# Local attention on one core: masks of the second scoring moved from matrix products into spare rows and GpSimd selects

## The chip, the core and the metric

One Trainium2 chip; the kernel uses 1 of its cores. The metric is the device time of one execution in microseconds. The engines are TensorE (PE, with its weight loads as PEld), VectorE (DVE), ScalarE (ACT), GpSimd (POOL), and SyncE (SP), which issues the DMAs here. The engines run on their own and meet at semaphores.

## The reference

A sequence of 4096 tokens of width 256 goes through a global causal attention on one side and two layers of "local attention, then gated MLP" on the other; the two results are multiplied. Only the local attention changes. Cut to what matters (4096 tokens, 8 heads of 64, a window of 128):

```python
def local_attention(q, k, v):                  # once in each of 2 layers
    w = n // WINDOW
    bq = q.reshape(b, h, w, WINDOW, d) * QK_SCALE
    ...
    bk, bv = (look_around(bk), look_around(bv))        # previous and own window
    sim = jnp.einsum('bhwid,bhwjd->bhwij', bq, bk)
    mask = (i < j) | (i > j + WINDOW) | (j == -1)
    sim = jnp.where(mask, -jnp.finfo(sim.dtype).max, sim)
    attn = jax.nn.softmax(sim, axis=-1)
    out = jnp.einsum('bhwij,bhwjd->bhwid', attn, bv)
```

A query sees its own window up to itself, and of the window before it the part from the same offset on. So each window of keys is seen by two windows of queries, each through a triangle.

## The kernel before

`local_attention_layer` holds everything that changes. It works on 16 pairs of windows (32 windows of 128 tokens, `NT`), in a hand-written software pipeline: every engine runs `for k in range(NI + 4)`, and in iteration k it works on several stages of different pairs. The order in which the calls stand in each engine's loop is the order in which that engine runs them; only semaphores tie the engines together.

Scores are made twice. `score_max(w)` makes them with queries on partitions: a mask by four products of an identity with a stored mask (`mask_unit`, L1094: 128x512 bf16, one for each of four PSUM banks of `SU`), then the query-key products (L1109). DVE's `row_max` takes the maxima (L1315) and writes their negative in two parts, high and low, to `msp` (L1323, L1325); PE transposes `msp` (L1147), ACT copies the result to `negm` (L1020). `score_turned(kb)` makes the scores again with keys on partitions, for the two query windows that see key window kb: again `mask_unit`, then products of `row1` with `negm` (L1126), which add the negative maxima, and then the query-key products (L1133). ACT takes the exponential to `PT` (`weights`, L1012), two instructions for each window, for four heads each. PE's `weigh` multiplies `PT` with `V` and with ones (L1211).

The products of `score_max` and `score_turned` use 32 of PE's 128 rows each, four of them side by side. In `msp` each group of 32 rows after the transpose holds the two parts of the maxima and 30 rows of zeros; `row1` has ones in the first two rows of each group and zeros in the rest. The windows are stored in a ring of six (`RW = 6`), so the two query windows of kb are next to each other except when kb modulo 6 is 5; then `spans` splits the products into two runs.

One iteration has two halves. In the **odd half** PE runs score_max(2k-3), the transposes of the input (L1226), weigh(k-4, 1), score_turned(2k-5), a broadcast (L1242), the transpose of the maxima (L1147), values(2k) (L75 to L77 into B6) and then the output projection (L75 to L77 with `woh`). That last one waits for ACT's copy of the values out of B6 (L1027) and for POOL's `oTl` (L974). In the **even half** it runs the query and key projections, score_max(2k-2), more projections, values(2k+1), score_turned(2k-4), the sums of squares (L1277), the transpose of the maxima, the transposes of the sums (L1285, which wait for ACT's copy `sse`, L1081), and weigh(k-3, 0).

DVE runs in the odd half: the maxima (L1315), L1323, L1325, a copy of one column (L1365) and a subtraction (L1368), then the reciprocal (L1348) and the product `on` (L1352) for the pair k-4, and the scaling of queries and keys (L1379). ACT follows: the high part of `on` (L1040), the two exponentials of window 2k-5, `negm`, and the copy of the values. POOL has `low_part` (L974, a subtraction), the four rotary additions (L987) and the power (L993); in time, the power of iteration k is followed by low_part(k-3, 0), and in iteration k+1 by low_part(k-3, 1).

Of the kernel before, what the change touches and what calls it, by code (L numbers as in the profile page):

```python
# [6 lines left out]
F32 = mybir.dt.float32  # L7
# [6 lines left out]
P = 128  # L14
# [853 lines left out]

def local_attention_layer(nc, layer, X, w_qkv, w_o, rope, scale_cols, ident, identb, window_mask):

    with ExitStack() as ctx:
# [22 lines left out]
        ones = sb("ones", [P, HQ])  # L895
        row1 = sb("row1", [P, P], F32R)
        tab = sb("tab", [P, 4, N2])
# [15 lines left out]
        on = sb("on", [P, OC, N2])  # L913
        oT_hi, oT_lo = (sb(f"oT{i}", [P, OC, N2], F32R) for i in "hl")
        stage = PT[:, 0:2, :, :].rearrange("p a b c -> p (a b c)")

# [3 lines left out]
        B7 = psum("B7", [P, 512])  # L920

        const_in, wq_in, wo_in = sem("const_in"), sem("wq_in"), sem("wo_in")
        wh_done, wl_done, set_done, nsc_done = sem("wh_done"), sem("wl_done"), sem("set_done"), sem("nsc_done")
# [8 lines left out]
        def live(k):  # L932
            return 0 <= k < NI
# [15 lines left out]
        @block.sync  # L949
        def _(sp):  # L950
            sp.dma_start(stage[:, 0:EC * 3 * INNER], w_qkv).then_inc(wq_in, 16)
            for dst, src in ((id_sb[:, :], ident), (idb_sb[:, :], identb), (mask[:, :], window_mask), (sc_sb[:, :], scale_cols)):
                sp.dma_start(dst, src).then_inc(const_in, 16)
            sp.wait_ge(wh_done, 1)
            sp.wait_ge(wl_done, 1)
            sp.dma_start(stage[:, 0:OC * E], w_o).then_inc(wo_in, 16)
            for k in range(NI):
                if k >= 1:
                    sp.wait_ge(rope_done, 16 * k)
                sp.dma_start(tab[:, :, :], rope[:, k, :, :]).then_inc(tab_in, 16)  # L960

        @block.gpsimd
        def _(pool):
            pool.memset(half[:, :], -0.5).then_inc(half_set, 1)
            pool.memset(msp[:, :, :, :, :].rearrange("p a b c d -> p (a b c d)").bitcast(F32), 0.0).then_inc(set_done, 1)
            pool.memset(ones[:, :], 1.0).then_inc(set_done, 1)
            pool.wait_ge(half_set, 1)

            def low_part(p, q):
                if live(p):  # L970
                    pool.wait_ge(ohi_done, 2 * p + q + 1)
                    if p >= 1:
# [4 lines left out]
                                       ).then_inc(olo_done, 1)  # L977

            for k in range(NI + 4):
                low_part(k - 4, 1)  # L980
                if live(k):
                    for g in range(4):
                        n = 4 * k + g
                        pool.wait_ge(rope_done, 4 * (n + 1))
                        if k >= 1:
                            pool.wait_ge(nrm_done, 2 * (k - 1) + g // 2 + 1)
                        pool.tensor_tensor(rot[:, g, :, :].rearrange("p a b -> p (a b)"),  # L987
                                           t[:, n % 2, 0, :, :].rearrange("p a b -> p (a b)"),
                                           t[:, n % 2, 1, :, :].rearrange("p a b -> p (a b)"), ALU.add).then_inc(rot_done, 1)
                    pool.wait_ge(ssc_done, k + 1)  # L990
                    if k >= 1:
                        pool.wait_ge(rnx_done, k)
                    pool.tensor_tensor(rn[:, :, :, :].rearrange("p a b c -> p (a b c)"),  # L993
                                       ssc[:, :, :, :].rearrange("p a b c -> p (a b c)"), half[:, :], ALU.pow).then_inc(rn_done, 1)
                low_part(k - 3, 0)

        @block.scalar
        def _(act):
# [4 lines left out]
            act.wait_ge(wl_done, 2)  # L1003
            act.wait_ge(set_done, 10)

# [80 lines left out]
        def _(pe):  # L1086
            pe.wait_ge(const_in, 64)
            pe.wait_ge(wh_done, 2)
            pe.wait_ge(wl_done, 2)
            pe.wait_ge(set_done, 10)  # L1090

# [22 lines left out]
            def score_turned(kb):  # L1114
# [72 lines left out]
            def weigh(p, q):  # L1187
# [103 lines left out]
        def _(dve):  # L1291
            dve.memset(blocks[:, :], 0.0).then_inc(clear_done, 1)
            dve.memset(row1[:, :].bitcast(F32), 0.0).then_inc(clear_done, 1)
            dve.wait_ge(clear_done, 2)
            for i in range(4):
                dve.memset(blocks[32 * i:32 * i + 32, i:i + 1], 1.0).then_inc(set_done, 1)
                dve.memset(row1[32 * i:32 * i + 2, :].bitcast(F32), 1.0).then_inc(set_done, 1)
# [3 lines left out]
            dve.wait_ge(const_in, 64)  # L1301
            dve.tensor_scalar(nsc[:, :], sc_sb[:, :], -1.0, None, ALU.mult).then_inc(nsc_done, 1)
            dve.wait_ge(wh_done, 2)
# [3 lines left out]
            dve.wait_ge(set_done, 10)  # L1307

# [384 lines left out]
def build(nc, t, out, stop=99):  # L1693
# [17 lines left out]
    for layer in range(DEPTH):  # L1711
        n = str(layer)
        local_attention_layer(nc, layer, X, t["w_lqkv" + n], t["w_lo" + n], t["rope"], t["rope_scale" + n], t["ident"],
                              t["identb"].bitcast(BF16), t["window_mask"].bitcast(BF16))
        mlp_layer(nc, layer, X, t["w_1" + n], t["w_2" + n], t["b_1" + n], t["ln" + n], t["b_2" + n], t["ident"],
                  t["shift"], t["carry"])
# [3 lines left out]
def lay_out(inp):  # L1720
# [58 lines left out]
    both = np.concatenate([np.where(c < r, MASKED, 0.0), np.where(c > r, MASKED, 0.0)], 1)  # L1779
    arr["window_mask"] = bf16_bits(np.tile(both, (1, 2)))  # L1780
    arr["shift"] = (c == r + 1).astype(np.float32)
    arr["carry"] = ((r == P - 1) & (c == 0)).astype(np.float32)
# [14 lines left out]
```

## Time and profile before

| | |
|---|---|
| time, median of 3 runs | 3600.45 us (3595.33 to 3605.28) |
| the profiled execution | 3591.3 us, of which its span is 3589.6 us |
| PE busy | 88% |
| DVE busy | 66% |
| ACT busy | 48% |
| POOL busy | 22% |
| first local attention, from the load of its weights to the load of the MLP's | 1783.8 to 2391.6 us |
| its steady loop | about 34.5 us for one of the iterations 4 to 15 |

The page gives each engine's busy share. In its 40 slices the local attention stands in slices 20 to 26 and 30 to 36. A timeline lists the instructions of an engine in order of time: start, length, engine, line, operation, tiles, shapes, how many were merged into the row, and in brackets how long the engine was idle before it and who ended that. Records of matmuls can be missing: of 512 mask products 386 are in the trace.

### The profile page before, as it was taken

Reading aid. Unit: us, or ns where it says so; the run is one execution under the profiler, and the core shown is the slowest. Engines: PE = TensorE matmul, PEld = TensorE weight load, DVE = VectorE, ACT = ScalarE, POOL = GpSimd, SP = SyncE. Lnnn points to the kernel's source line nnn. Section 1 sums busy time; section 2 is a strip of 40 time slices with the busy share of each in tenths; the row PEclk is TensorE's granted clock in tenths of the full one; section 3 lists DMA queues with packets and bytes.
Section 4 is the critical chain, followed back from the end, with each engine's and each line's share of the span. In section 5 each row is a group of like instructions: output and inputs, shape, how many; then the busy total and the mean of one; then the engine's idle time right before and its main releaser. Section 6 shows DMA issues by size and latency. Waiting matters only on the chain. (4 is left out here: it accounts for less than half of the span.)

```text
span 3589.6 us, 75899 instructions
## 1 busy us (share of the span) xinstructions
PE 3172.1 (88%) x31726; PEld 1932.4 (54%) x31852; DVE 2376.7 (66%) x3284; ACT 1724.8 (48%) x3173; POOL 783.9 (22%) x757
## 2 busy tenths in 40 slices
PE   7799999999999999999679999959978999985995
PEld 6333333334433333333457777747766777764884
DVE  7698978987889977765246655635545556654554
ACT  4266777887678778777123333212213333321222
POOL 8410000000100000001034343302224333331221
PEclk9699999999999999989789999979989999997998
DMA  7420001000200000000310000000000000000003
GB/s 246 128 53 16 9 9 44 9 16 17 66 24 9 16 9 4 5 7 8 128 30 19 13 20 19 8 31 0 0 32 19 19 20 13 19 8 31 0 0 141
DMA packets 62014, 113.62 MB, mean 32 GB/s; under 512 B 9608, under 2 KB 25480, under 8 KB 61192
## 3 DMA queue, kind: packets, MB, share of 16 engines
q1 hardware_dynamic: 57608, 102.84, 9.3%
q10 hardware_dynamic: 4096, 6.30, 0.7%
q8 instruction: 237, 3.88, 0.5%
q14 instruction: 73, 0.60, 0.1%
HBM read 74.77 MB, written 33.55 MB: 30 GB/s over the span
## 5 line engine op out<-in xcount | busy, mean ns | idle before, releaser
L647 DVE TENSOR_REDUCE mp<-ps_m 128x2 f32<-128x1024 f32 (+3 forms) x1152 | 1281.1, 1134 | 245.4 <-PE ps_m L698 182.8
L623 ACT ACTIVATE probs<-ps_s 128x512 f32<-128x512 f32 (+3 forms) x2304 | 1161.5, 560 | 395.9 <-PE ps_s L722 366.3
L738 PE MATMUL ps_o<-probs,vall 128*32 128x256 f32 (+3 forms) x9216 | 715.6, 383 | 13.4 <-POOL probs L602 12.6
L722 PE MATMUL ps_s<-qst,kst 64*128 64x512 f32 (+3 forms) x2304 | 611.0, 491 | 39.0 <-ACT probs L623 23.7
L722 PEld LDWEIGHTS ps_s<-qst,kst 64*128 64x128 f32 x2304 | 243.3, 188 | 507.9 <-ACT probs L623 444.5
L698 PE MATMUL ps_m<-kst,qst 64*128 64x512 f32 (+3 forms) x2304 | 485.7, 400 | 31.7 <-DVE mp L647 14.1
L738 PEld LDWEIGHTS ps_o<-probs,vall 128*32 128x32 f32 x9216 | 186.6, 109 | 343.1 <-issue 207.8
L698 PEld LDWEIGHTS ps_m<-kst,qst 64*128 64x128 f32 x2304 | 236.7, 193 | 72.5 <-DVE mp L647 53.6
L987 POOL TENSOR_TENSOR a_rot<-a_t 128x512 f32<-128x512 f32 x128 | 163.0, 1274 | 448.0 <-DVE a_t L1342 448.0
L591 POOL TENSOR_TENSOR msplit<-negm,mzero 128x16 fp32r<-128x16 f32 x32 | 7.2, 224 | 1136.3 <-DVE negm L653 1136.3
L1512 ACT ACTIVATE m_gl<-m_bank_u,m_b 128x512 f32<-128x512 f32 x96 | 66.1, 688 | 345.0 <-PE m_bank_u L77 345.0
L1033 ACT ACTIVATE a_sq<-a_BP 128x512 f32<-128x512 f32 x128 | 76.6, 598 | 292.1 <-PE a_BP L77 292.1
L1342 DVE SCALAR_TENSOR_TENSOR a_t<-a_BP,a_sc,a_tab 128x256 f32<-128x256 f32 x384 | 166.8, 476 | 62.6 <-ACT a_sq L1033 62.4
L993 POOL TENSOR_TENSOR a_rn<-a_ssc,a_half 128x32 f32<-128x32 f32 x32 | 174.0, 5438 | 94.2 <-DVE a_ssc L1399 94.2
L1040 ACT ACTIVATE a_oTh<-a_on 128x512 fp32r<-128x512 f32 x64 | 40.4, 631 | 300.1 <-DVE a_on L1352 300.1
L75 PE MATMUL m_bank_u<-m_hh,m_w1h 128*128 128x512 f32 x384 | 156.0, 406 | 28.3 <-DVE m_uf L1619 28.3
L1348 DVE RECIPROCAL a_rec<-a_B 128x256 f32<-128x256 f32 x64 | 112.2, 1754 | 100.3 <-PE a_B L1211 99.8
L1315 DVE TENSOR_REDUCE a_mx<-a_SU 128x4 f32<-128x1024 f32 (+1 forms) x128 | 148.6, 1202 | 39.2 <-PE a_SU L1109 39.2
L602 POOL TENSOR_SCALAR_AFFINE_SELECT probs<-probs 128x256 f32<-128x256 f32 x256 | 101.9, 406 | 331.2 <-ACT probs L623 331.1
L1012 ACT ACTIVATE a_PT<-a_SU 128x1024 f32<-128x1024 f32 (+1 forms) x128 | 122.4, 1008 | 106.1 <-PE a_SU L1133 106.1
L1491 POOL TENSOR_TENSOR m_ul<-m_uf,m_uh 128x512 fp32r<-128x512 f32 x96 | 126.2, 1315 | 195.0 <-DVE m_uh L1625 195.0
L76 PE MATMUL m_bank_u<-m_hl,m_w1h 128*128 128x512 f32 x384 | 153.0, 398 | 0.0
(182 smaller groups left out, 5241.2 us busy)
## 6 DMA issues: line engine op xcount, KB each, us to landing
a_tab<-in_rope SPq DMA_DIRECT2D x32, 512.0 KB
q_parts<-pparts SPq DMA_DIRECT2D x32, 256.0 KB, 3.9
k_parts<-pparts SPq DMA_DIRECT2D x32, 256.0 KB, 3.8
qst<-q_parts SPq DMA_DIRECT2D x64, 128.0 KB, 2.7
o_raw<-o_sb SPq DMA_DIRECT2D x32, 256.0 KB, 2.0
X<-in_x SPq DMA_DIRECT2D x8, 512.0 KB, 7.3
kst<-k_parts SPq DMA_DIRECT2D x32, 128.0 KB, 3.7
qst<-q_parts SPq DMA_DIRECT2D x64, 64.0 KB, 2.6
```

What stands on the lines that cost most here:

```text
L75: pe.matmul(out, a_hi, b_hi, start=start, stop=False)
L76: pe.matmul(out, a_hi, b_lo, start=False, stop=False)
L623: act.activation(probs[:, s % PR, h, off:C], sslots[n % SR][:, off:C], ACT.Exp, scale=float(D) ** -0.5).then_inc(exp_done, 1)
L647: dve.tensor_reduce(mp[b % 2][:, h:h + 2, cc:cc + 1], slot[:, :, 0:width], AX.X, ALU.max).then_inc(max_read, 1)
L698: last = pe.matmul(slot[:, x, 0:width], qst[q_slot(b)][rows, hp, a * P:(a + 1) * P], kst[g % 2][rows, hp, cc * C:cc * C + width], start=Tr ...
L722: pe.matmul(sslots[n % SR][:, off:C], kst[g % 2][rows, hp, i * P:(i + 1) * P], qst[q_slot(b)][rows, hp, off:C], start=True, stop=True).the ...
L738: last = pe.matmul(ps_o[32 * h:32 * h + VW, lo:hi], vall[:, i, (g * GH + h) * DV:(g * GH + h) * DV + VW], probs[:, s % PR, h, lo:hi], star ...
L987: pool.tensor_tensor(rot[:, g, :, :].rearrange("p a b -> p (a b)"), t[:, n % 2, 0, :, :].rearrange("p a b -> p (a b)"), t[:, n % 2, 1, :, ...
L993: pool.tensor_tensor(rn[:, :, :, :].rearrange("p a b c -> p (a b c)"), ssc[:, :, :, :].rearrange("p a b c -> p (a b c)"), half[:, :], ALU. ...
L1315: dve.tensor_reduce(mx[:, w % 2, 2 * b:2 * b + 2, :], SU[:, 2 * b:2 * b + 2, :].rearrange("p i (q c) -> p i q c", q=2)[:, :, :, lo:N2], AX ...
L1342: dve.scalar_tensor_tensor(out=dst, in0=src, scalar=s, in1=table, op0=ALU.mult, op1=ALU.mult).then_inc(rope_done, 1)
L1491: pool.tensor_tensor(u_lo[:, m, :], uf[:, m % 2, :], u_hi[:, m, :].bitcast(F32), ALU.subtract).then_inc(ul_done, 1)
```

## The change

`score_turned` no longer calls `mask_unit`. Three things take its place.

- A staircase mask in the rows that were zero. A new table comes in by one more DMA. `msp` is no longer set to zero but to a table whose columns 2 to 17 hold -1e30 where the query's block of eight tokens matches the column; after the transpose these are 16 more rows beside the maxima in `negm`. `row1` becomes two stationary operands: `rows_own` for the key's own window and `rows_next` for the next one, with ones in rows 2 to 17 where a key's block of eight lies wholly on the masked side. Since the two differ, the product is made per query window: 16 products of 128 columns where there were 8 of 256 (where the ring split them there were 16 of 128 already). The first of them in each bank starts the accumulation.
- What the staircase leaves, triangles of eight by eight, is set to zero after the exponential by GpSimd: `trim(kb, b)` is two affine_selects on 128x512 elements each, in place in `PT` (one in the last window).
- `weigh` waits for `trim_done`, which counts these selects.

`score_max` keeps its mask. The setup loses a memset on POOL and five on DVE and gains three copies on DVE.

```diff
@@ the loads
             for dst, src in ((id_sb[:, :], ident), (idb_sb[:, :], identb), (mask[:, :], window_mask), (sc_sb[:, :], scale_cols),
+                             (table, window_rows)):
@@ gpsimd
+            def trim(kb, b):
+                if win(kb):
+                    pool.wait_ge(exp_done, 2 * kb + b + 1)
+                    part = PT[:, kb % PR, 2 * b:2 * b + 2, :].rearrange("p i (q c) -> p (i q) c", q=2)
+                    own = pool.affine_select(part[:, :, 0:P], part[:, :, 0:P], pattern=[[0, 4], [1, P]], compare_op=ALU.is_ge,
+                                             fill=0.0, base=0, channel_multiplier=-1)
+                    own.then_inc(trim_done, 1)
+                    if kb + 1 < NT:
+                        pool.affine_select(part[:, :, P:N2], part[:, :, P:N2], pattern=[[0, 4], [-1, P]], compare_op=ALU.is_ge,
+                                           fill=0.0, base=0, channel_multiplier=1).then_inc(trim_done, 1)
             for k in range(NI + 4):
                 low_part(k - 4, 1)
+                trim(2 * k - 6, 1)
+                trim(2 * k - 5, 0)
                 if live(k):
                     for g in range(4):
+                        if g == 2:
+                            trim(2 * k - 5, 1)
...
+                else:
+                    trim(2 * k - 5, 1)
+                trim(2 * k - 4, 0)
                 low_part(k - 3, 0)
@@ tensor
             def score_turned(kb):
...
-                mask_unit()
-                for q in range(2):
-                    for at, off, n in runs:
+                for part, rows_by in enumerate((rows_own, rows_next)[0:2 if kb + 1 < NT else 1]):
+                    at = ((kb + part) % RW) * P
+                    for q in range(2):
                         for i in range(4):
                             rows = slice(32 * i, 32 * i + 32)
-                            pe.matmul(SU[:, i, q * N2 + off:q * N2 + off + n], row1[rows, :], negm[rows, q, at:at + n],
-                                      start=False, stop=False, tile_position=(32 * i, 0), skip_group_check=True)
+                            pe.matmul(SU[:, i, q * N2 + part * P:q * N2 + part * P + P], rows_by[rows, :], negm[rows, q, at:at + P],
+                                      start=(part == 0 and q == 0), stop=False, tile_position=(32 * i, 0), skip_group_check=True)
@@ weigh
                     pe.wait_ge(exp_done, 2 * (2 * p + 2))
+                    pe.wait_ge(trim_done, min(4 * (2 * p + 2), 4 * NT - 2))
@@ vector, setup
+            dve.tensor_copy(rows_own[:, :], table[:, 0:P]).then_inc(set_done, 1)
+            dve.tensor_copy(rows_next[:, :], table[:, P:2 * P]).then_inc(set_done, 1)
+            dve.tensor_copy(msp[:, :, :, :, :].rearrange("p a b c d -> p (a b c) d"), ...
```

On PE, at the score_turned of an even half, between the last products of the values and the first of weigh, there stands before:

```order
L77 MATMUL a_B<-a_wqh,a_hTl 128x512
L1094 MATMUL a_SU<-a_mask,a_idb 128x512 x4
L1126 MATMUL a_SU<-a_negm,a_row 128x256 x8
L1133 MATMUL a_SU<-a_QK 128x256 x16
L1277 MATMUL a_B<-a_sq,a_blocks 32x256 x8
L1147 MATMUL a_B<-a_id,a_msp 128x128 x2
L1285 MATMUL a_B<-a_id,a_sse 128x128 x2
```

and now, with rowso for `rows_own` and rowsn for `rows_next`:

```order
L77 MATMUL a_B<-a_wqh,a_hTl 128x512
L1146 MATMUL a_SU<-a_negm,a_rowso 128x128 x8
L1146 MATMUL a_SU<-a_negm,a_rowsn 128x128 x8
L1153 MATMUL a_SU<-a_QK 128x256 x16
L1298 MATMUL a_B<-a_sq,a_blocks 32x256 x8
L1167 MATMUL a_B<-a_id,a_msp 128x128 x2
L1306 MATMUL a_B<-a_id,a_sse 128x128 x2
```

The four mask products are gone and the row products are twice as many at half the width; nothing else on PE moved.

On POOL, from the low parts of one iteration of the steady loop to the rotary additions of the one after the next, it read before:

```order
L974 TENSOR_TENSOR a_oTl<-a_on,a_oTh 128x512 x2
L987 TENSOR_TENSOR a_rot<-a_t 128x512 x4
L993 TENSOR_TENSOR a_rn<-a_ssc,a_half 128x32
L974 TENSOR_TENSOR a_oTl<-a_on,a_oTh 128x512 x2
L987 TENSOR_TENSOR a_rot<-a_t 128x512 x4
```

and one iteration reads now:

```order
L1004 TENSOR_TENSOR a_rot<-a_t 128x512 x2
L1010 TENSOR_TENSOR a_rn<-a_ssc,a_half 128x32
L985 AFFINE_SELECT a_PT<-a_PT 128x4x128
L989 AFFINE_SELECT a_PT<-a_PT 128x4x128
L976 TENSOR_TENSOR a_oTl<-a_on,a_oTh 128x512 x2
L985 AFFINE_SELECT a_PT<-a_PT 128x4x128
L989 AFFINE_SELECT a_PT<-a_PT 128x4x128
L985 AFFINE_SELECT a_PT<-a_PT 128x4x128
L989 AFFINE_SELECT a_PT<-a_PT 128x4x128
L1004 TENSOR_TENSOR a_rot<-a_t 128x512 x2
L985 AFFINE_SELECT a_PT<-a_PT 128x4x128
L989 AFFINE_SELECT a_PT<-a_PT 128x4x128
```

Two selects came between the power and the low parts, four between the low parts and the rotary additions, and two between the second and the third of these.

## Rows read from the trace of the kernel before

**Rows 1.** Busy time by stage: PE, PEld, DVE, ACT, POOL, then granted clock, DMA, GB/s

```profile
1835.00:2283.00 448.00, 414.84 (x5486) 320.04 (x5536) 264.61 (x452) 143.46 (x234) 175.27 (x92) 1.00 0.06 18
...
2723.00:3170.00 447.00, 413.84 (x5465) 319.03 (x5511) 263.72 (x450) 144.83 (x235) 174.61 (x92) 1.00 0.06 18
```

**Rows 2.** One line by itself, the mask products: ns of one, min/median/max

```profile
L1094 PE MATMUL a_SU<-a_mask,a_idb x386: 379/379/389, 1834.3 to 3252.8; 128*128 128x512 bf16 x193
```

**Rows 3.** Timeline, even half, PE then ACT: start, us long, engine, line [idle before]

```profile
2029.05 0.81 PE L1094 MATMUL a_SU<-a_mask,a_idb 128*128 128x512 bf16 x3
2029.79 0.51 PE L1126 MATMUL a_SU<-a_negm,a_row 32*128 32x256 f32 x8
2030.13 1.89 PE L1133 MATMUL a_SU<-a_QK 32*128 32x256 f32 x32
2034.37 0.44 PE L1285 MATMUL a_B<-a_id,a_sse 128*128 128x128 f32 x2 [0.98 <-ACT a_sse L1081]
...
2032.10 1.94 ACT L1012 ACTIVATE a_PT<-a_SU 128x1024 f32<-128x1024 f32 x2 [2.49 <-PE a_SU L1133]
2033.93 0.39 ACT L1081 ACTIVATE a_sse<-a_B 128x256 f32<-128x256 f32 x1
```

**Rows 4.** Timeline, odd half, PE

```profile
2044.69 0.67 PE L1126 MATMUL a_SU<-a_negm,a_row 32*128 32x128 f32 x16
...
2045.19 2.00 PE L1133 MATMUL a_SU<-a_QK 32*128 32x128 f32 x64
...
2050.60 0.36 PE L75 MATMUL a_B<-a_woh,a_oTh 128*128 128x256 f32 x1 [0.78 <-ACT a_V L1027]
```

**Rows 5.** Timeline, odd half: DVE, ACT and POOL, in order of time

```profile
2035.12 5.44 POOL L993 TENSOR_TENSOR a_rn<-a_ssc,a_half 128x32 f32<-128x32 f32 x1 [3.21 <-DVE a_ssc L1399]
...
2040.53 2.36 DVE L1315 TENSOR_REDUCE a_mx<-a_SU 128x4 f32<-128x1024 f32 x2 [0.43 <-PE a_SU L1109]
...
2040.85 1.27 POOL L974 TENSOR_TENSOR a_oTl<-a_on,a_oTh 128x512 fp32r<-128x512 f32 x1 [0.29 <-ACT a_oTh L1040]
...
2042.92 0.18 DVE L1323 TENSOR_SCALAR a_msp<-a_mx 128x8 fp32r<-128x8 f32 x1
...
2043.13 0.17 DVE L1325 SCALAR_TENSOR_TENSOR a_msp<-a_mx,a_msp 128x8 fp32r<-128x8 f32 x1
...
2043.91 1.75 DVE L1348 RECIPROCAL a_rec<-a_B 128x256 f32<-128x256 f32 x1
...
2049.10 0.39 ACT L1020 ACTIVATE a_negm<-a_B 128x256 fp32r<-128x256 f32 x1
...
2049.86 0.60 ACT L1027 ACTIVATE a_V<-a_B 128x512 f32<-128x512 f32 x1 [0.37 <-PE a_B L77]
```

**Rows 6.** One line by itself, POOL: the selects of the global attention, ns min/median/max

```profile
L602 POOL TENSOR_SCALAR_AFFINE_SELECT probs<-probs x256: 403/406/416, 159.2 to 1716.7; 128x256 f32<-128x256 f32 x128
```

**Rows 7.** Groups by line, POOL: the rotary additions (count, busy, mean ns, idle before)

```profile
L987 POOL TENSOR_TENSOR a_rot<-a_t 128x512 f32<-128x512 f32 x128 | 163.0, 1274 | 448.0 <-DVE a_t L1342 448.0
```

**Rows 8.** Timeline, inner loop of the MLP: DVE copies beside a GpSimd subtraction

```profile
2445.53 0.43 DVE L1625 CAST m_uh<-m_uf 128x512 fp32r<-128x512 f32 x1
...
2445.93 1.85 DVE L1632 CAST m_hh<-m_hf 128x512 fp32r<-128x512 f32 x2
...
2446.03 1.46 POOL L1491 TENSOR_TENSOR m_ul<-m_uf,m_uh 128x512 fp32r<-128x512 f32 x1 [1.50 <-DVE m_uh L1625]
```

**Rows 9.** Timeline, third iteration: the same DVE steps beside the power

```profile
1843.67 5.44 POOL L993 TENSOR_TENSOR a_rn<-a_ssc,a_half 128x32 f32<-128x32 f32 x1 [0.65 <-DVE a_ssc L1399]
...
1848.63 0.18 DVE L1323 TENSOR_SCALAR a_msp<-a_mx 128x8 fp32r<-128x8 f32 x1
```

**Rows 10.** Timeline, drain, PE

```profile
2353.83 0.38 PE L75 MATMUL a_B<-a_woh,a_oTh 128*128 128x256 f32 x1 [0.84 <-POOL a_oTl L974]
```

**Rows 11.** Timeline, start of the first layer: the weights from issue to use

```profile
1783.75 0.33 SPq L951 DMA_DIRECT2D a_PT<-in_w_lqkv  x1
...
1790.43 2.76 ACT L1000 ACTIVATE a_wqh<-a_PT 128x3072 fp32r<-128x3072 f32 x1 [64.99 <-DMA a_PT<-in_w_lqkv]
```

More of the change, by code:

```diff
@@ L866, in _, with local_attention_layer @@
                                       bo_sb[:, :].rearrange("p (o e) -> p o e", o=1).broadcast_to([P, 2, E]), ALU.add).then_inc(y_out, 1)
-def local_attention_layer(nc, layer, X, w_qkv, w_o, rope, scale_cols, ident, identb, window_mask):
+def local_attention_layer(nc, layer, X, w_qkv, w_o, rope, scale_cols, ident, identb, window_mask, window_rows):
     with ExitStack() as ctx:
@@ L895, in local_attention_layer @@
         ones = sb("ones", [P, HQ])
-        row1 = sb("row1", [P, P], F32R)
+        rows_own, rows_next = (sb(f"rows{i}", [P, P], F32R) for i in "on")
         tab = sb("tab", [P, 4, N2])
@@ L914, in local_attention_layer @@
         oT_hi, oT_lo = (sb(f"oT{i}", [P, OC, N2], F32R) for i in "hl")
+        table = sq[:, 0, :, :].rearrange("p a b -> p (a b)")[:, 0:2 * P + HQ]
         stage = PT[:, 0:2, :, :].rearrange("p a b c -> p (a b c)")
@@ L920, in local_attention_layer @@
         B7 = psum("B7", [P, 512])
+        trim_done = sem("trim")
         const_in, wq_in, wo_in = sem("const_in"), sem("wq_in"), sem("wo_in")
@@ L951, in _ @@
             sp.dma_start(stage[:, 0:EC * 3 * INNER], w_qkv).then_inc(wq_in, 16)
-            for dst, src in ((id_sb[:, :], ident), (idb_sb[:, :], identb), (mask[:, :], window_mask), (sc_sb[:, :], scale_cols)):
+            for dst, src in ((id_sb[:, :], ident), (idb_sb[:, :], identb), (mask[:, :], window_mask), (sc_sb[:, :], scale_cols),
+                             (table, window_rows)):
                 sp.dma_start(dst, src).then_inc(const_in, 16)
@@ L1003, in _ @@
             act.wait_ge(wl_done, 2)
-            act.wait_ge(set_done, 10)
+            act.wait_ge(set_done, 8)
             def weights(kb):
@@ L1086, in _ @@
         def _(pe):
-            pe.wait_ge(const_in, 64)
+            pe.wait_ge(const_in, 80)
             pe.wait_ge(wh_done, 2)
             pe.wait_ge(wl_done, 2)
-            pe.wait_ge(set_done, 10)
+            pe.wait_ge(set_done, 8)
             def mask_unit():
@@ L1292, in _ @@
             dve.memset(blocks[:, :], 0.0).then_inc(clear_done, 1)
[L1293 to L1294 removed]
+            dve.wait_ge(clear_done, 1)
             for i in range(4):
                 dve.memset(blocks[32 * i:32 * i + 32, i:i + 1], 1.0).then_inc(set_done, 1)
[L1297 removed]
             dve.wait_ge(wh_done, 1)
@@ L1300, in _ @@
                               wq_hi[:, :, :].rearrange("p a b -> p (a b)").bitcast(F32), ALU.subtract).then_inc(wl_done, 1)
-            dve.wait_ge(const_in, 64)
+            dve.wait_ge(const_in, 80)
             dve.tensor_scalar(nsc[:, :], sc_sb[:, :], -1.0, None, ALU.mult).then_inc(nsc_done, 1)
+            dve.tensor_copy(rows_own[:, :], table[:, 0:P]).then_inc(set_done, 1)
+            dve.tensor_copy(rows_next[:, :], table[:, P:2 * P]).then_inc(set_done, 1)
+            dve.tensor_copy(msp[:, :, :, :, :].rearrange("p a b c d -> p (a b c) d"),
+                            table[:, 2 * P:2 * P + HQ].rearrange("p (o d) -> p o d", o=1).broadcast_to([P, 16, HQ])
+                            ).then_inc(set_done, 1)
             dve.wait_ge(wh_done, 2)
@@ L1306, in _ @@
             dve.wait_ge(nsc_done, 1)
-            dve.wait_ge(set_done, 10)
+            dve.wait_ge(set_done, 8)
             def row_max(w):
@@ L1780, in lay_out @@
     arr["window_mask"] = bf16_bits(np.tile(both, (1, 2)))
+    block = np.arange(P) // 8
+    rows_own, rows_next = np.zeros((32, P), np.float32), np.zeros((32, P), np.float32)
+    rows_own[0:2], rows_next[0:2] = 1.0, 1.0
+    rows_own[2:18] = block[None, :] > np.arange(16)[:, None]
+    rows_next[2:18] = block[None, :] < np.arange(16)[:, None]
+    hot = np.zeros((P, 32), np.float32)
+    hot[:, 2:18] = np.where(block[:, None] == np.arange(16)[None, :], MASKED, 0.0)
+    arr["window_rows"] = np.ascontiguousarray(np.concatenate([np.tile(rows_own, (4, 1)), np.tile(rows_next, (4, 1)), hot], axis=1))
     arr["shift"] = (c == r + 1).astype(np.float32)
```

3 lines of the change are left out of this document (1 added, 2 removed).

## Prediction

> **What bounds the kernel now.** The page's first section first, whose shares stand in the table of the time before: PE 88%, no other engine over 66%. The busy table by stage says it more sharply for the two loops that the change touches: PE is busy 415 of 448 us in one and 414 of 447 us in the other, at a granted clock of 1.00 all through, with DVE at 264 and POOL at 175 us [rows 1]. So these loops are PE's, and what leaves PE's queue counts, but only where nothing else is waited for right behind it. That the busy table can't say; the timeline of one iteration can. In the even half PE runs without a gap into score_turned and then stops for 0.98 us for ACT's copy `sse`; ACT itself stood idle for 2.49 us until score_turned ended, then ran two exponentials and that copy [rows 3]. That pause therefore hangs on the end of score_turned and moves with it. In the odd half PE stops for 0.78 us ahead of the output projection, for ACT's copy of the values [rows 4]. Here ACT comes from elsewhere: DVE's maxima start at 2040.53, the reciprocal at 2043.91, `negm` on ACT ends at 2049.49, and the copy of the values starts at 2049.86, having waited 0.37 us for PE [rows 5]. Between, ACT takes the high part of DVE's product ahead of the exponentials, so its queue is fed by DVE and not by score_turned. This chain starts with score_max, ahead of the edit.
>
> **What leaves PE.** Three recorded mask products take 0.81 us, and one takes 0.379 [rows 2, 3], so they follow each other every (0.81 - 0.379) / 2 = 0.2155 us, and four are 0.86 us. The fourth isn't in the record; the row products start 0.74 us after the first recorded one [rows 3], which is three steps and 0.09 us of change-over, and the change-over stays. The row products grow from 8 of 256 columns, 0.34 us from 2029.79 to 2030.13 [rows 3], to 16 of 128; the trace has that shape too, where the ring splits them: 0.50 us from 2044.69 to 2045.19 [rows 4]. That is 0.16 us more (none for the five odd windows that are split already). Net: 0.70 us less PE for each score_turned.
>
> **The even half** gets all of it. Exponentials, `sse` and its transposes come 0.70 us earlier, since ACT was idle. There are 16 such windows in a layer (0, 2, ... 30): 16 x 0.70 = 11.2 us.
>
> **The odd half** gets little. PE comes 0.70 us earlier to its wait, but the copy of the values can start at best when ACT is free, 0.37 us earlier [rows 5]. The rest becomes pause: 0.78 + 0.33 = 1.11 us. This holds for the 12 windows 3 to 25. Window 1 has no such wait and gets 0.70. Windows 27, 29 and 31 get nothing: in the drain PE waits there for POOL's `oTl`, 0.84 us in the one shown [rows 10], at the end of the same DVE chain.
>
> **What POOL gets.** A select of 128x256 takes 406 ns [rows 6]. The new ones have twice the elements, so 0.81 us if it scales from zero and some 0.71 if 0.1 us of it is fixed (an estimate); I take 0.76. The far bound is the subtraction of the same 512 elements with two inputs, 1.27 us [rows 5]. Eight of them are 6.1 us in an iteration of 34.5 in which POOL has 175/448 = 39% of busy time [rows 1]: there is room, so the question is only the place of each. The pair between the rotary additions and the four behind the low parts stand ahead of additions that wait for DVE anyway, 448 us for 128 of them or 3.5 us each [rows 7]; the even half's `weigh` asks for selects that stand two additions ahead of the power, so long done. They cost nothing as long as four of them, 3 us, fit between the low parts and the first addition, and if they didn't, each us too many would delay DVE's use of its two `t` buffers. The first pair is different. It goes between the power, which ends at 2035.12 + 5.44 = 2040.56, and low_part(k-3, 0), which ran from 2040.85 to 2042.12 [rows 5]. With the pair ahead of it low_part ends at 2040.56 + 2 x 0.76 + 1.27 = 2043.35, with the gaps between some 2043.4. Nobody waits for this low part so early. But DVE's small steps L1323 and L1325 start at 2042.92 and 2043.13 [rows 5], until now just behind it, and now beside it.
>
> Do DVE's SBUF steps stand still beside a GpSimd operation? In the MLP, yes: a copy of 128x512 takes 0.43 us, and two of them beside a GpSimd subtraction of 1.46 us took 1.85 instead of 0.86; the last one began where that subtraction ended, at about 2047.4 [rows 8]. Beside the power, no: L1323 took its 0.18 us there [rows 9]. The low part is a subtraction like the one in the MLP, so I take the held case: L1323 begins at 2043.4 and not at 2042.92, and DVE's chain, the one that bounds the odd half, is 0.45 us late (0.38 to 0.58 with selects of 0.71 to 0.81; 0 if not held). The Trainium skill states this as a rule that speaks against the change (SBUF — State Buffer, section "SBUF: two separate sides"): the port pair that VectorE and GpSimd share is an exclusive lock held for a whole instruction, and it is taken by a DVE instruction in a two-port mode or, against a GpSimd instruction that reads SBUF, by one with two SBUF inputs. 
>
> So the odd half comes to 0.37 - 0.45 = -0.08 us: 12 x -0.08 = -1.0, window 1 gives +0.7, and window 27, where the power is still there in the drain, loses about 0.3. Sum of the odd half: -0.6 us a layer.
>
> **Setup.** The three DVE copies (128x512 at most, so each under the 0.43 us of rows 8 and its like) stand where DVE waits for the load of `w_o`, and so cost nothing; without that cover it would be 1 us a layer. The added DMA is 0.15 MB behind the 1.57 MB of `w_lqkv`, which took 6.7 us from issue to use [rows 11]: 0 if they go one after the other, 9% of 6.7 = 0.6 us if they share. I take 0.25 us a layer.
>
> **The sum.** A layer: 11.2 - 0.6 - 0.25 = 10.3 us; two layers: 20.7 us. Against the profiled execution: 3591.3 - 20.7 = 3570.6. That execution was 9 us under the median of the runs, so against the median: 3600.45 - 20.7 = 3580, which is 0.6% faster. What measurement can tell from no change here is about 0.3%, 11 us.
>
> **Rival 1: DVE is not held.** Tiny steps slip through as beside the power. Then the odd half keeps its 0.37: 13 x 0.45 = 5.9 us more a layer, 3568. For it: rows 9. Against it: rows 8.
>
> **Rival 2, the other side: the first pair of selects is long.** Four separate rows of 128 with a stride may run like a two-input operation. Place: between the power and low_part(k-3, 0); price: each select counts twice, 26 times in two layers, through DVE's held chain, so 0.1 us more of length costs 5.2 us. At 1.27 us low_part ends at 2044.4, DVE is 1.47 us late, and the sum is -20.7 + 26 x 1.02 = +6: 3606. It decides from 0.76 + 20.7/52 = 1.16 us on. Against it: rows 7, an operation of the same kind on two such rows. Half way to it, selects of 0.95 to 1.08 us give 3580 + 52 x (0.19 to 0.32) = 3590 to 3597.
>
> **Rival 3: the clock.** The pause ahead of the output projection grows from 0.78 to 1.1, with the hold 1.6 us. The granted clock was 1.00 through both loops with pauses of 0.8 and 1.0 us in each iteration [rows 1, 3, 4]. If it fell to 1.2 GHz now, 20.7 / 24 = 0.86 us of PE work at that level in each steady iteration would eat the gain; a few times that much gives 3620. The Trainium skill (TensorE: Matmul & The Clock Gate, "A second HAM failure mode: psum-queue depth-cycling") tells of short idle spells between groups of matmuls that make the clock swing between its two levels. By that rule the time would be this rival's; the rows at 1.00 so far speak against it.
>
> **That the even half's gain is hidden** is the last one: some later DVE or POOL step bounds it after all. I find none, since ACT's 2.49 us of idleness is ended by PE, but it would leave only the odd half and the setup: 3600 + 2 x 0.85 = 3602.
>
> **Chances.** Forecast (3574 to 3587) 0.50; rival 1 0.22; rival 2 0.06 in full and 0.09 half way; rival 3 0.04; even gain hidden or lost elsewhere 0.09. The range is 3560 to 3597: it takes in the forecast, rival 1 with some noise below it, and rival 2 half way. Faster by over 0.3% (under 3590): 0.76. Within: 0.15. Slower: 0.09.
>
> **What would show it.** In the new profile: 256 mask products left instead of 512 (fewer are recorded); score_turned 0.70 us shorter; the pause ahead of the output projection 1.1 us or more, that ahead of `sse` unchanged at 0.98; selects of 0.71 to 0.81 us; L1323 in the odd half beginning where low_part(k-3, 0) ends; the clock at 1.00. The iteration would be 0.6 us shorter (held) or 1.07 (not held). I am wrong if PE waits for `trim_done` anywhere, if selects pass 1.1 us, or if DVE's reciprocal begins as early after the maxima as before (3.38 us from 2040.53 to 2043.91).

## The result and the profile after

The changed kernel takes 3562.43 us (median of 6 runs, 3556.87 to 3576.12) where the one before took 3601.64 (6 runs, 3595.33 to 3605.28). The ratio is 0.9899, with a 95% interval of 0.9880 to 0.9919: faster by 1.0%, or 29 to 43 us. The prediction was 3580 us in a range of 3560 to 3597. The direction holds, and the time lies in the range by 2 us; the gain is almost twice the 20.7 us forecast, and the time lies nearer to rival 1 (3568). The profiled execution took 3556.87 us, 34.4 less than the one of before.

The page's head and the busy table of the same stretches as [rows 1] come first (columns as there):

```profile
span 3555.1 us, 76617 instructions
...
PE 3139.6 (88%) x32012; PEld 1927.2 (54%) x32012; DVE 2378.4 (67%) x3280; ACT 1720.0 (48%) x3173; POOL 931.3 (26%) x1007
```

```profile
1835.00:2283.00 448.00, 416.54 (x5786) 328.86 (x5788) 275.08 (x466) 148.03 (x244) 238.15 (x196) 1.00 0.06 18
2723.00:3170.00 447.00, 418.93 (x5887) 330.40 (x5889) 272.85 (x460) 148.58 (x243) 238.66 (x198) 1.00 0.06 17
```

PE's share is what it was, the granted clock is 1.00 in both loops, so rival 3 is out, and of the columns only POOL's has moved much, from 175 to 238 us (DVE's by some 10). Since the share doesn't tell where the time went, the timelines have to. First the even half on PE, to be laid beside [rows 3]:

```profile
2021.68 0.45 PE L1146 MATMUL a_SU<-a_negm,a_rowso 32*128 32x128 f32 x8
2021.95 0.39 PE L1146 MATMUL a_SU<-a_negm,a_rowsn 32*128 32x128 f32 x8
2022.18 1.95 PE L1153 MATMUL a_SU<-a_QK 32*128 32x256 f32 x32
...
2026.47 0.33 PE L1306 MATMUL a_B<-a_id,a_sse 128*128 128x128 f32 x1 [0.98 <-ACT a_sse L1101]
```

No mask products, row products of 0.50 us, and the same pause of 0.98 us behind. Then the odd half, for [rows 4] and [rows 5]: PE, DVE, POOL and ACT, each in order of time.

```profile
2035.82 0.45 PE L1146 MATMUL a_SU<-a_negm,a_rowso 32*128 32x128 f32 x8
...
2041.87 0.36 PE L75 MATMUL a_B<-a_woh,a_oTh 128*128 128x256 f32 x1 [0.92 <-ACT a_V L1047]
...
2032.63 2.36 DVE L1339 TENSOR_REDUCE a_mx<-a_SU 128x4 f32<-128x1024 f32 x2 [0.42 <-PE a_SU L1129]
2035.02 0.17 DVE L1347 TENSOR_SCALAR a_msp<-a_mx 128x8 fp32r<-128x8 f32 x1
2035.23 0.17 DVE L1349 SCALAR_TENSOR_TENSOR a_msp<-a_mx,a_msp 128x8 fp32r<-128x8 f32 x1
...
2036.00 1.75 DVE L1372 RECIPROCAL a_rec<-a_B 128x256 f32<-128x256 f32 x1
...
2032.62 0.63 POOL L985 TENSOR_SCALAR_AFFINE_SELECT a_PT<-a_PT 128x512 f32<-128x512 f32 x1
2033.21 0.63 POOL L989 TENSOR_SCALAR_AFFINE_SELECT a_PT<-a_PT 128x512 f32<-128x512 f32 x1
2033.81 1.28 POOL L976 TENSOR_TENSOR a_oTl<-a_on,a_oTh 128x512 fp32r<-128x512 f32 x1
...
2039.05 1.92 ACT L1032 ACTIVATE a_PT<-a_SU 128x1024 f32<-128x1024 f32 x2
2040.86 0.38 ACT L1040 ACTIVATE a_negm<-a_B 128x256 fp32r<-128x256 f32 x1
2041.12 0.61 ACT L1047 ACTIVATE a_V<-a_B 128x512 f32<-128x512 f32 x1
```

Three things are to be seen. A select takes 0.63 us and the next one starts after 0.59, so the record of the low part ends at 2033.81 + 1.28 = 2035.09. DVE's L1347 starts at 2035.02, 0.07 us before that end, and takes its usual 0.17 us: of the 0.45 us that the forecast priced nothing is left (in iterations 5 to 14 the two lie 0.04 to 0.10 us over each other). The reciprocal comes 3.37 us after the maxima, as before (3.38), which the prediction had named as a sign that it is wrong. And the copy of the values now starts 0.26 us after `negm` does, without waiting for PE; PE idles 0.92 us for it, against 0.78.

Measured by the starts of the power, one of which stands in each iteration, the steady iteration fell from 34.63 to 33.28 us (22 intervals in the two layers, of the iterations 4 to 15), by 1.35 us. PE's rows split this: from the output projection to the sums of squares (even) 16.15 to 15.47 us, so -0.68; from the first query-key product of score_max to the output projection (odd) 11.99 to 11.32, so -0.67; the stretch between them stays at 6.5. The forecast had -0.70 and +0.08.

### The profile page after: what moved, and what is told of

Read it like the earlier page. It is cut to its first block and busy times, and to the rows that moved or that the text cites. A ratio compares the mean times of both kernels' runs of the same rounds, so it can differ in the third digit from the quotient of the medians.

```text
span 3555.1 us, 76617 instructions
## 1 busy us (share of the span) xinstructions
PE 3139.6 (88%) x32012; PEld 1927.2 (54%) x32012; DVE 2378.4 (67%) x3280; ACT 1720.0 (48%) x3173; POOL 931.3 (26%) x1007
## 5 line engine op out<-in xcount | busy, mean ns | idle before, releaser
L1339 DVE TENSOR_REDUCE a_mx<-a_SU 128x4 f32<-128x1024 f32 (+1 forms) x128 | 148.7, 1203 | 39.2 <-PE a_SU L1129 39.2
```

Of the source, the lines that this page charges most:

```text
L1339: dve.tensor_reduce(mx[:, w % 2, 2 * b:2 * b + 2, :], SU[:, 2 * b:2 * b + 2, :].rearrange("p i (q c) -> p i q c", q=2)[:, :, :, lo:N2], AX ...
```

## Experiments

The table has the level of each: the steady iteration, the sum over both layers of the time from the first power to the sixteenth, and the ratio to the kernel before in runs on the same chip. Columns two and three come from the one profiled execution, and leave out the global attention ahead, which no kernel here touches and which is the larger part of the scatter: the load of the first layer's weights, behind it, is issued anywhere from 1777.4 (e10_pair_late) to 1809.2 us (e8_stair_pair_late).

| kernel | iteration, us | both layers, us | ratio to before (95%) |
|---|---|---|---|
| before | 34.63 | 983.0 | |
| changed | 33.28 | 952.7 | 0.9899 (0.9880 to 0.9919) |
| after_again | 33.28 | 948.8 | 0.9917 (0.9887 to 0.9946) |
| e1_mask_even | 34.16 | 976.0 | 0.9995 (0.9978 to 1.0011) |
| e2_mask_odd | 34.10 | 970.6 | 0.9977 (0.9963 to 0.9992) |
| e3_selects_only | 34.62 | 983.6 | 1.0028 (1.0011 to 1.0046) |
| e4_pair_twice | 34.39 | 979.6 | 1.0002 (0.9982 to 1.0021) |
| e5_v_first | 33.12 | 946.6 | 0.9916 (0.9884 to 0.9949) |
| e6_stair_max | 32.62 | 932.7 | 0.9868 (0.9838 to 0.9898) |
| e7_stair_low_first | 32.68 | 932.6 | 0.9860 (0.9818 to 0.9902) |
| e8_stair_pair_late | 32.16 | 920.4 | 0.9800 (0.9773 to 0.9827) |
| e9_stair_late_v | 31.89 | 914.3 | 0.9776 (0.9747 to 0.9805) |
| e10_pair_late | 33.27 | 951.2 | 0.9889 (0.9860 to 0.9918) |

**How large is each half?** In the changed kernel, the mask goes back into one half (`== 1` for the odd one):

```diff
+                if kb % 2 == 0:
+                    mask_unit()
...
-                                      start=(part == 0 and q == 0), stop=False, ...
+                                      start=(part == 0 and q == 0 and kb % 2 != 0), stop=False, ...
```

> The changed kernel, with the four mask products put back ahead of the row products of score_turned in the even half only (the selects stay, so what they zero is masked twice). The changed kernel is 39 us under the one before. If the two halves add up and the even half gives its full PE time, as the prediction had it and as the trace of the changed kernel reads (0.88 us less from score_max to the row products' end, 32 such windows in two layers), this run gives 0.86 to 0.95 x 32 = 28 to 30 us back: 3590 to 3593 us, and the iteration grows by 0.9 us. Rival: the even half's gain comes out of something else (fewer waits elsewhere), then it gives back under 20 us.

> The changed kernel, with the four mask products put back ahead of the row products of score_turned in the odd half only. Theory A, read from the two traces: the odd half gained 0.56 us in most iterations and 0.84 where the ring splits the products, though the prediction gave it -0.08; then putting the mask back costs 0.56 to 0.84 x 24 and something at the ends, 15 to 18 us: 3577 to 3581 us. Theory B, as predicted: ACT's copy of the values, at the end of DVE's chain, bounds the odd half, and most of what PE got there was pause; then it costs 0 to 5 us: 3562 to 3568, and the missing gain lies elsewhere.

In the even half the mask costs 0.88 us an iteration, as said; over both layers 23 us in the loops (27 against after_again). The odd half is at the upper end of theory A: 0.82 us an iteration and 18 us in the loops (22 against after_again). Theory B, the prediction's own, is out. Both masks together cost 1.70 us, and the change gained 1.35; the 0.35 between them are the split row products. In e1_mask_even that price can be read alone, since its even half differs on PE from the one of before by nothing else: from the row products to the sums of squares 2.38 us against 2.17, so 0.21, of which 0.16 are the row products and 0.05 the score products behind them. The medians came out higher than expected, 3597.65 and 3590.29 us; in the profiled executions, which lie within 1 us of them, the first power stood 9 and 11 us later than in that of the changed kernel.

**Are the selects free?** Selects and the wait of `weigh` in the kernel before, with all masks kept:

```diff
+                trim(2 * k - 6, 1)
+                trim(2 * k - 5, 0)
...
+                trim(2 * k - 4, 0)
                 low_part(k - 3, 0)
...
+                    pe.wait_ge(trim_done, min(4 * (2 * p + 2), 4 * NT - 2))
```

> The kernel before with nothing but the GpSimd selects and the wait of weigh for them added (all mask products stay, so the selects zero what is zero already). Selects take 0.64 us, so the first pair and the low part behind it end some 0.2 us before DVE's small steps L1323 and L1325. If POOL's part is free: 3600 to 3603, no change. If the pair delays DVE by the 0.45 us of the prediction in each iteration: 26 x 0.45 = 12 us more, 3612.

Free: the loops take 983.6 us against 983.0 and the iteration 34.62 against 34.63. The pair and the low part end as they do in the changed kernel: L1343, the step that is L1347 there, starts 0.07 to 0.10 us before that end in iterations 5 to 14 and takes its 0.17 to 0.18 us.

The median is 3607.18 us, above the 3600 to 3603 expected for this case, and the interval of the ratio (1.0011 to 1.0046) leaves out 1. The profiled execution took 10.6 us more than that of before, and 9.1 of them stand ahead of the first power (1829.9 against 1820.8 us), before the first select has run. So that part isn't the price of the selects; a small price outside the loops isn't ruled out by these runs.

**Is DVE held at all?** The pair runs twice in the changed kernel, the second pair behind the first:

```diff
                 trim(2 * k - 4, 0)
+                if win(2 * k - 4):
+                    part = PT[:, (2 * k - 4) % PR, 0:2, :].rearrange("p i (q c) -> p (i q) c", q=2)
+                    for lo, sign in ((0, 1), (P, -1)):
+                        pool.wait_ge(trim_done, 4 * (2 * k - 4) + (1 if lo == 0 else 2))
+                        pool.affine_select(part[:, :, lo:lo + P], part[:, :, lo:lo + P], ...).then_inc(again_done, 1)
                 low_part(k - 3, 0)
```

> The changed kernel, with the first pair of selects (between the power and the low part) run twice; the second pair waits for the first and zeroes the same elements again, so low_part(k-3, 0) ends 1.2 us later and lies over DVE's small steps L1347 and L1349. This is the overlap that the prediction feared and that the shorter selects just avoided. If a DVE step with SBUF operands stands still beside a GpSimd subtraction (the forecast's case): L1347 begins where the low part ends, some 1.1 us later, the reciprocal too, and with 24 to 26 iterations the time goes up by 20 to 30 us: 3583 to 3592. If only L1349 with its two SBUF inputs is held: the same within 0.2 us an iteration. If neither is held: 3562 to 3565.

POOL and DVE in an odd half:

```profile
2046.42 1.23 POOL L1019 TENSOR_SCALAR_AFFINE_SELECT a_PT<-a_PT 128x512 f32<-128x512 f32 x2
2047.61 1.28 POOL L976 TENSOR_TENSOR a_oTl<-a_on,a_oTh 128x512 fp32r<-128x512 f32 x1
...
2047.65 1.27 DVE L1354 TENSOR_SCALAR a_msp<-a_mx 128x8 fp32r<-128x8 f32 x1
2048.96 0.17 DVE L1356 SCALAR_TENSOR_TENSOR a_msp<-a_mx,a_msp 128x8 fp32r<-128x8 f32 x1
```

It is held, and in a way that the record shows as a long instruction and not as a late one: L1354 (L1347 in the changed kernel) takes 1.27 us instead of 0.17 and ends at 2048.92, 0.03 us after the record of the subtraction (2048.89). The iteration grew by 1.11 us, the delay's 1.10 to a hundredth, and the loops by 27 us (31 against after_again). The median, 3597.11 us, is 35 us above the changed kernel's and over the 3583 to 3592 expected; what is more than the loops' part wasn't traced. So the price per us of delay in the prediction (all of it passes through to the iteration) was right, and so was the mechanism; only the collision didn't take place. The step has one SBUF input and one SBUF output. By the rule that the prediction took from the Trainium skill (SBUF — State Buffer, section "SBUF: two separate sides") such a step is held if it runs in a two-port mode; the hold agrees with that, but no run here shows the mode.

**A control.**

> The changed kernel unchanged, as the level for the three runs beside it. In the traces of the four runs before, the work ahead of the first local attention, which no kernel here touches, took 6 to 11 us longer than in the two traces shown first. If that comes from the chip or the moment, this run shows it too, its time lies at 3562 to 3571 us, and the steady iteration stays at 33.3 us. If it belongs to the edited kernels, this run gives 3562 and its first power starts at 1819 us as before.

The iteration is again 33.28 us, and the first power stands at 1825.6. Most of the scatter lies ahead of the loops, in work that is the same in every kernel. The 948.8 against 952.7 us go with the clock in the second layer of the first trace: in the 78 us from its first power PE was granted 0.87 of full speed there, 0.93 in this trace and in that of before, and the first three iterations of that layer took 3.8 us more than those of the first.

**What bounds the odd half?**

```diff
-                if win(2 * k - 3):
-                    turn_max(2 * k - 3)
                 if live(k):
                     take_v(2 * k)
+                if win(2 * k - 3):
+                    turn_max(2 * k - 3)
```

> The changed kernel with two steps of ACT exchanged in the odd half: the copy of the values (L1047) ahead of `negm` (L1040). The theory: the output projection waits for ACT's copy of the values, which stands at the end of the chain from DVE's maxima over the reciprocal and the exponentials; in the changed kernel it starts 0.26 us after `negm` does, 10.57 us after score_max starts, with PE idle for 0.97 us. If this chain bounds the odd half, the copy and the output projection come 0.26 us earlier (the values are there 10.3 us after score_max starts), the iteration is 0.2 to 0.26 us shorter and the time 5 to 6 us. Rival: the odd half is bound by PE or by something else behind; then nothing changes (0 to 1 us), or `negm`, now later, delays PE and the time grows.

The iteration lost 0.17 us, so ACT's end of the chain does bound the changed kernel's odd half. It is less than 0.26, because the copy then met the values, which PE has ready just then:

```profile
2039.35 1.93 ACT L1032 ACTIVATE a_PT<-a_SU 128x1024 f32<-128x1024 f32 x2
2041.29 0.60 ACT L1047 ACTIVATE a_V<-a_B 128x512 f32<-128x512 f32 x1
...
2042.03 0.36 PE L75 MATMUL a_B<-a_woh,a_oTh 128*128 128x256 f32 x1 [0.78 <-ACT a_V L1047]
```

Elsewhere ACT starts its next step 0.1 us before the record of the one before ends; here it doesn't. PE's pause is back at 0.78 us, as in [rows 4]. So 0.78 is the pause when PE's own values come last; what is above it (0.92 here, 0.97 on average) is ACT's chain. The ratio can't tell this run from the changed kernel; what is said here rests on the iterations.

**Does the collision decide elsewhere?** A change that moves DVE's steps towards POOL's. In score_max:

```diff
-                mask_unit()
+                for q in range(2):
+                    for i in range(4):
+                        rows = slice(32 * i, 32 * i + 32)
+                        pe.matmul(SU[:, i, q * N2:(q + 1) * N2], steps[rows, :], stairs[rows, :], start=(q == 0), ...
```

`stairs` holds rows_next and rows_own side by side, `steps` the -1e30 of each block of eight, from 128 more columns of the table.

> The changed kernel, and in score_max too the four mask products are replaced, here by eight products of 32 rows and 256 columns that add the same staircase (the maxima then run over up to seven masked keys more, which changes no softmax, only the shift). Eight such products take 0.34 us, so score_max is 0.95 - 0.34 = 0.6 us shorter, twice in an iteration. The even half is PE's and gets its 0.6 us: 32 x 0.6 = 19 us less in all. The odd half decides: DVE's L1347 would come 0.6 us earlier, but the first pair of selects and the low part on POOL come from the power and stay where they are, and the low part ends 0.07 us after L1347 starts now. Theory (DVE's small step is held while GpSimd subtracts): L1347 ends where the low part ends, the reciprocal starts no earlier, and the odd half gets 0 to 0.1 us: 3562 - 19 = 3543 us, or 0.5% less than the changed kernel. Rival (the small steps are not held): both halves get 0.6 us, 64 x 0.6 = 38 us: 3524 us.

> The same kernel as e6_stair_max with one more edit: on POOL low_part(k-3, 0) stands ahead of the first pair of selects, so that it ends 1.27 us behind the power and not 2.46. If the holding is the cause that keeps the odd half's gain in e6_stair_max, L1347 runs in 0.17 us again and this run is 0.5 to 0.6 us an iteration shorter than that one, 12 to 15 us in all: 3524 to 3531 us. If a select holds the step as a subtraction does (the pair now lies where the low part was), it gains nothing over e6_stair_max. If the small steps are not held at all, both runs are alike too, at 3524.

The iteration fell by 0.66 us in e6_stair_max. The even half gave 0.62, the odd half the rest, as the holding theory had it. POOL and DVE in an odd half:

```profile
2033.78 1.28 POOL L978 TENSOR_TENSOR a_oTl<-a_on,a_oTh 128x512 fp32r<-128x512 f32 x1
...
2034.46 0.63 DVE L1354 TENSOR_SCALAR a_msp<-a_mx 128x8 fp32r<-128x8 f32 x1
```

Held up to 2035.09, again 0.03 us after the record of the subtraction (2035.06). But e7_stair_low_first, which moves the subtraction out of the way, gained nothing. The same places there:

```profile
2042.39 1.29 POOL L978 TENSOR_TENSOR a_oTl<-a_on,a_oTh 128x512 fp32r<-128x512 f32 x1 [0.29 <-ACT a_oTh L1062]
2043.63 0.64 POOL L987 TENSOR_SCALAR_AFFINE_SELECT a_PT<-a_PT 128x512 f32<-128x512 f32 x1
2044.22 0.64 POOL L991 TENSOR_SCALAR_AFFINE_SELECT a_PT<-a_PT 128x512 f32<-128x512 f32 x1
...
2043.95 0.35 DVE L1354 TENSOR_SCALAR a_msp<-a_mx 128x8 fp32r<-128x8 f32 x1
2044.34 0.55 DVE L1356 SCALAR_TENSOR_TENSOR a_msp<-a_mx,a_msp 128x8 fp32r<-128x8 f32 x1
```

A select holds as a subtraction does: L1354 ends at 2044.30, 0.03 us after the record of the first (2044.27), and L1356 at 2044.89, as much after that of the second (2044.86). I had expected 12 to 15 us from this run and named this outcome as the other possibility. If selects hold too, the pair has to leave the place altogether, and the next run tests that:

```diff
                 low_part(k - 4, 1)
+                trim(2 * k - 6, 0)
                 trim(2 * k - 6, 1)
...
-                trim(2 * k - 4, 0)
                 low_part(k - 3, 0)
```

> The kernel of e6_stair_max with the first pair of selects taken out from between the power and low_part(k-3, 0) and put an iteration later, behind low_part(k-4, 1), where four selects stand already. In e6_stair_max the small DVE step L1354 lasted until the low part ended, in e7_stair_low_first L1354 and L1356 each lasted until a select ended; either way 0.5 to 0.65 us. If selects hold these steps as the subtraction does, nothing is left here to hold them: L1354 takes its 0.17 us, the reciprocal starts 3.37 us after the maxima and not 3.8 to 3.9, and the iteration is 0.4 to 0.5 us shorter than in e6_stair_max, 32.15 us; the time is 10 to 12 us under that run. If the delay in e7_stair_low_first came from anything else (PSUM, ACT's copy, the input's transposes), the steps stay long or the reciprocal late, and the iteration stays at 32.6 us.

> The kernel of e8_stair_pair_late and the exchange of e5_v_first on ACT (the copy of the values ahead of `negm`). Alone that exchange gave 0.18 us an iteration of 0.26 expected, since PE's values then came last. Here PE idles 0.4 us more ahead of the output projection than there would be without the chain, so it should again give 0.1 to 0.2 us an iteration: 32.0 us, 2 to 5 us in all. This is the version meant to beat both kernels: about 1.1% under the changed kernel, 2.1% under the one before.

> The changed kernel with only the pair moved as in e8_stair_pair_late. In the changed kernel the low part ends 0.02 to 0.07 us beside L1347, which took its 0.17 us. If the holding is all that this place costs, the move gains nothing here, the iteration stays at 33.3 us within 0.05 (and the six selects behind low_part(k-4, 1), 3.6 us, fit ahead of the first rotary addition). If the pair costs something else in its old place, the iteration is shorter; if six selects in a row are too many, DVE's rotary steps are late and it is longer.

The iterations of the first and the third came out as written, that of the second a little better; in the medians e8_stair_pair_late is 13 us under e6_stair_max (10 to 12 expected; 12.3 in the loops). In e8_stair_pair_late DVE's steps are short again,

```profile
2022.49 1.29 POOL L978 TENSOR_TENSOR a_oTl<-a_on,a_oTh 128x512 fp32r<-128x512 f32 x1 [0.28 <-ACT a_oTh L1062]
...
2021.67 2.35 DVE L1346 TENSOR_REDUCE a_mx<-a_SU 128x4 f32<-128x1024 f32 x2
2024.05 0.17 DVE L1354 TENSOR_SCALAR a_msp<-a_mx 128x8 fp32r<-128x8 f32 x1
2024.26 0.17 DVE L1356 SCALAR_TENSOR_TENSOR a_msp<-a_mx,a_msp 128x8 fp32r<-128x8 f32 x1
```

and the iteration is 32.16 us, 0.46 less than in e6_stair_max. The exchange on ACT gives 0.27 more (31.89), a little above the 0.1 to 0.2 expected: the chain is the later one by more, and the copy starts 0.12 us before the exponentials' record ends (2042.59 against 2042.70), so PE's values were there. PE's pause is 0.80 us on average, against 1.06. In e10_pair_late the same move gains nothing (33.27), since in the changed kernel the pair holds nothing in its old place.

e9_stair_late_v is the fastest: 3523.94 us (3516.77 to 3530.12), 0.9776 of the kernel before (0.9747 to 0.9805) and clearly under the changed one. One caveat is argued and not tested by any run, for e6_stair_max to e9_stair_late_v: the maxima include up to seven masked keys, so a query whose masked neighbour scores some 87 above all its visible keys would have a sum of zero. Whoever takes it over has to know the bounds of the scores.

## Why the prediction was right, and where not

That the time fell in the range is in part luck. Two terms of the forecast's odd half were wrong, both so that the gain came out too small; they are told below. The iteration lost 1.35 us, where the prediction had 0.62 with the hold and 1.07 without; and the range reached down to 3560 for the sake of rival 1, whose reason is false.

**PE's terms** held. 0.86 us for four mask products, 0.16 for the row products: the even half was forecast at -0.70 and measured -0.68. The parts were less exact than the sum: the mask is worth 0.88 (0.97 from score_max to the row products of the odd half, where a change-over goes too), and the split costs 0.21, not 0.16.

**The even half's cover** held: the pause before `sse` is 0.98 as before, and e1_mask_even gives its 0.88 us back, so its gain wasn't hidden, which puts the last rival out. Rival 2 is out too: a select takes 0.64 us.

**DVE's hold of 0.45 us** failed, and it was a size and not the mechanism. I took 0.76 us for a select, between 0.71 and 0.81 worked out from a 128x256 one [rows 6]. They take 0.64 and follow each other every 0.59 us. DVE's L1347 starts 2.36 us after the end of the power in both kernels; I had the low part end 2.84 us after it, and it ended after 2.43. The iterations of e3_selects_only and e10_pair_late show that the pair costs nothing there, e4_pair_twice that a us more would have cost its us. Rival 1 had the size of this (0.45 us less an iteration), but its reason, that small steps slip through, is false for a subtraction and a select.

**V's room of 0.37 us** failed too, and this I should have read. I put the earliest start of the copy at the end of `negm`'s record, 2049.49. ACT's records overlap: in [rows 3] `sse` starts at 2033.93 and the exponentials before it end at 2034.04. In the changed kernel the copy starts 0.26 us after `negm` starts, not 0.39. Counted so, the room was 0.50. Besides, I took one window for all, and [rows 4] and [rows 5] show one of the four in twelve where the ring splits the products. There the exponentials too had waited for PE, in the trace of the kernel before by 0.23 us,

```profile
2047.27 1.95 ACT L1012 ACTIVATE a_PT<-a_SU 128x1024 f32<-128x1024 f32 x2 [0.23 <-PE a_SU L1133]
```

and PE gained more, since its row products were split already; these got 0.84 us instead of the usual 0.56 to 0.60. The mean was 0.67.

Together: 0.45 for the hold and 0.30 for the room are 0.75 us in 24 iterations, 18 us. With these the forecast of 20.7 would have been 39 us. The medians differ by 39.2; the two profiled executions by 34.4, in which the second layer's clock took about 4 back.

**Small terms.** PE's waits for POOL's `oTl`, 8 of them, rose from 16.0 to 21.4 us in all: what PE gained ahead of them, in the drain, turned into pause, as said. The setup's price was put at 0.25 us a layer, and none is seen: from the load of the weights to the first power it took 37.1 and 37.4 us before, and 37.1 and 36.5 now. PE didn't wait for `trim_done`, neither in the steady loop nor in the drain. Its waits from 1900 to 2300 us are these three (total, times, longest):

```profile
PE a_B L1306 <- ACT a_sse L1101: 11.7, 12, 1.0
PE a_B L75 <- ACT a_V L1047: 11.6, 12, 1.1
PE a_BP L1263 <- DVE a_on L1376: 0.9, 1, 0.9
```

The selects and L1347 as lines by themselves, with ns min/median/max:

```profile
L985 POOL TENSOR_SCALAR_AFFINE_SELECT a_PT<-a_PT x128: 627/636/655, 1873.9 to 3222.6; 128x512 f32<-128x512 f32 x128
```

```profile
L1347 DVE TENSOR_SCALAR a_msp<-a_mx x64: 174/175/757, 1836.2 to 3200.7; 128x8 fp32r<-128x8 f32 x64
```

Not every L1347 got away: once in each layer, in iteration k = 4 (at 1901.23 and 2773.03 us), it took 0.76 us. In the kernel before, the maximum was 0.18.

## What to carry to other kernels

Where two engines' steps pass each other by tenths of a us, a forecast needs start-to-start distances of each shape; take them from repeats of the same instruction, not from the records' lengths, which overlap. When an operation goes onto GpSimd, look which small DVE steps with SBUF operands on both sides run at that moment, and put it where DVE reads PSUM (its maxima weren't held here) or waits. An engine's pause before a wait has two parts: the hand-over that is always there (0.78 us here) and what the chain behind it is late; only the second can be won.

## What the runs showed of the hardware

- A select on GpSimd over 128x512 fp32 takes 0.636 us, 0.59 from start to start; over half the elements 0.406 [rows 6]. An estimate from these two: 0.18 us of it is fixed and 0.9 ns go to a column. A subtraction of 128x512 with two inputs takes 1.28.
- DVE steps from SBUF to SBUF, of 8 elements a partition, stand still under a GpSimd subtraction and under a select, up to the end of the instruction that runs, and the record shows it as their length (0.35, 0.55, 0.63 and 1.27 us for 0.17). Beside the power of 5.44 us they didn't [rows 9]; why that one lets them pass stays open.
- DVE's maxima, which read PSUM, weren't held: two took 2.36 us with two selects and a subtraction beside them, as before without (L1339, and L1315 in [rows 5]).
- Eight row-tiled products of 32 rows and 256 columns put a mask into the four banks in 0.34 us (e6_stair_max, from 2029.55 to 2029.89 us), where four full products of 512 columns took 0.86 (an estimate from the steps of 0.2155 us in [rows 3]) and 0.96 with the change-over behind them (score_max of the changed kernel, from 2029.59 to 2030.55).
